# A graph attention layer with residual layer norm on one core: attention mixes x before gcn_w instead of after it

## The chip, the core and the metric

The kernel runs on one core of a Trainium2 chip. Its time is the time of one launch on the device, in microseconds (us). Times inside a launch come from one profiled execution; "the span" is the stretch from its first to its last instruction.

## The reference

There are 128 graphs of 64 nodes with 384 features each, x[128, 64, 384], and an integer matrix adj[128, 64, 64] with ones on the diagonal. For each graph, with the embedding row e = table[adj]:

```
hi = x @ W1[:384] + e @ W1[384:] + b1          # for each pair (i, j)
hj = x @ W2[:384] + e @ W2[384:] + b2
rel = sum(hi * hj);  A = softmax(where(adj != 0, rel, -1e9))
h   = relu((A @ x) @ gcn_w + gcn_b)
out = layernorm(x + h @ Wo + bo)
```

With adj only 0 or 1, the scores are x M x^T plus a term of the column, plus a term of the row u.x + k, where M, u and k are made once from the weights. A second, slower path in the kernel handles other values of adj; it does not run on these inputs and its few changed lines are left out below.

## The kernel before

The 8192 rows (tokens) are worked in 16 groups of 512: four pairs of graphs, 128 rows each. Every large product is made three times in a 4-byte format: a value is split into a high and a low part, and high x high, high x low and low x high are added in PSUM (`three`, L444). Before the loop come the weights: M = W1 W2^T (`m_stage`), the column term, the row term's column u (put beside gcn_w as columns 384 and 385 of `gcn_hi` and `gcn_lo`), and gcn_b laid out as a row by a matmul (`gb_row`).

TensorE's stages in a group are, in the order of `body`:
- `mix`: attention times the values of the group before, 96 matmuls of 64 columns; result in four banks;
- `score_stage`: 48 matmuls of 64 columns;
- `value` for the next group: x @ [gcn_w, u, u], 4 times 9 matmuls of 386 columns, which VectorE adds to gcn_b and stores as `hg_sb` (`value_out`);
- `out` of the group before: hidden rows times Wo, 4 times 9 matmuls of 384 columns;
- `turn`: transposes the attention weights;
- `proj` for the next group: M times x^T, 27 matmuls of 512 columns, which ScalarE stores as `gt_sb` (`project_out`).

ScalarE splits off the high part of relu(mixed) (`hidden`), takes the exponentials (`weigh`), splits x (`split_x`), copies the row terms (`row_terms`). VectorE makes the low part of the hidden rows (`low_half`), adds the row terms and the mask to the scores and takes maxima, normalises the weights, and at the end of each body adds x to the output, takes statistics (`residual`), moments (`moments`), and normalises (`normalise`). GpSimd adds bo to x (`bias_x`, L1140), makes the mask (`mask`, L1136), makes the low part of x (`split_x`, L1131) and takes mean and variance to 1/std (`inverse_std`: L1149, L1151). SyncE issues the loads and stores. Each queue is in order; the orders are written out by hand, and the engines meet by counting semaphores. The bodies 0, 1, 14 and 15 are unrolled with small differences; 2 to 13 are a loop of six double bodies.

Of the kernel before, what the change touches and what calls it, by code (L numbers as in the profile page):

```python
# [52 lines left out]
def gnn_layernorm_kernel(nc, x, x_t, adj, adj_t, edge, biases, w1_t, w2_t, gcn_w, wo_w, wo_b, out):  # L53
# [8 lines left out]
    HW = HID + 2  # L62
    ROW = HID + 64
# [16 lines left out]
    with ExitStack() as ctx:  # L80
# [10 lines left out]
        wo_lo = sb("wo_lo", [P, C, HID], F32R)  # L91
        sb("gap0", [P, 48])
# [4 lines left out]
        sb("gap1", [P, 32])  # L97
        gcn_hi = sb("gcn_hi", [P, C, ROW], F32R)[:, :, 0:HW]
        gcn_lo = sb("gcn_lo", [P, C, ROW], F32R)[:, :, 0:HW]
        ident = sb("ident", [P, P])  # L100
        w1t_sb = sb("w1t_sb", [P, C, HID])
        w2t_sb = sb("w2t_sb", [P, C, HID + 1])
# [4 lines left out]
        b1_sb, b2_sb, gb_sb = (bias_sb[:, n * C:(n + 1) * C] for n in range(3))  # L107
        wob_sb = sb("wob_sb", [P, HID])
# [13 lines left out]
        hg_sb = sb("hg_sb", [P, 2, PAIRS, HID + 1])  # L122
# [9 lines left out]
        gb_diag = sb("gb_diag", [P, HID])  # L132
        gb_row = sb("gb_row", [P, HID + 1])
# [30 lines left out]
        edges = sb("edges", [P, NODES])  # L164

# [3 lines left out]
        PROJ_BANK = [bank[4], bank[2], bank[3]]  # L169
        MIX_BANK = ((6, 6, 4), (7, 7, 5))  # L170
        VALUE_BANK = bank[1:5]
        score = bank[0]
        M_BANK = bank[5:8]
        PROJ0_BANK = bank[5:8]
        PROJ1_BANK = [bank[5], bank[2], bank[3]]
        C_BANK = bank[3], bank[4]
        GB_BANK = bank[2]
# [9 lines left out]
        gcn_loaded = [sem(f"gcn_loaded{c}") for c in range(C)]  # L187
# [4 lines left out]
        x_loaded = [sem(f"x_loaded{i}") for i in range(2)]  # L192
        adj_loaded = [sem(f"adj_loaded{i}") for i in range(2)]
# [13 lines left out]
        zero_column = sem("zero_column")  # L207
# [3 lines left out]
        gb_diag_ready = sem("gb_diag_ready")  # L211
        gb_mm = sem("gb_mm")
        gb_row_ready = sem("gb_row_ready")
# [12 lines left out]
        u_hi_ready = sem("u_hi_ready")  # L226
        u_lo_ready = sem("u_lo_ready")
# [10 lines left out]
        value_mm = sem("value_mm")  # L238
        hg_ready = sem("hg_ready")
# [7 lines left out]
        mix_mm = sem("mix_mm")  # L247
        hshi = sem("hshi")
        hslo = sem("hslo")
# [50 lines left out]
        def out_bank(g, q):  # L300

            if static(g, LAST - 2) and HALVES <= q:
                return bank[q - 1]
            if static(g, LAST - 1):
                return bank[(3, 1, 2, 3)[q]]
            if static(g, LAST):
                return bank[q + 1]
            return bank[(5, 6, 7, 1)[q]]
# [5 lines left out]
        def x_home(g, slot):  # L314

            if static(g, LAST):
                return xt_sb[:, 0].rearrange("p c t -> p (c t)").rearrange("p (q d) -> p q d", d=HID)
            return x_sb[:, slot]

        def y_home(g, slot):  # L320

            if static(g, LAST):
                return xt_sb[:, 1].rearrange("p c t -> p (c t)").rearrange("p (q d) -> p q d", d=HID)
            return y_sb[:, slot]
# [42 lines left out]
        def _(sp):  # L367
# [11 lines left out]
            sp.dma_start(xt_sb[:, 0, :, GT // 2:GT], xt_cols[0][:, :, GT // 2:GT]).then_inc(xt_loaded[0], 16)  # L379
            sp.dma_start(xt_sb[:, 1], xt_cols[1]).then_inc(xt_loaded[1], 16)  # L380
            sp.dma_start(wob_sb[:], wo_b.to_broadcast([P, HID])).then_inc(wob_loaded, 16)
            sp.dma_start(wo_sb[:], wo_w.rearrange("(c p) n -> p c n", p=P)).then_inc(wo_loaded, 16)
            load_adj(0, 0)
            load_adj(1, 1)
            sp.dma_start(x_sb[:, 0], x_rows[0]).then_inc(x_loaded[0], 16)

            def body(g, par):

                if before(g, GROUPS - 2):
# [6 lines left out]
                if not static(g, 0):  # L396
                    if before(g, LAST - 1):
# [852 lines left out]
```

## Time and profile before

| | |
|---|---|
| time, median of 3 runs | 381.94 us (381.56 to 383.81) |
| the profiled execution's own time | 381.69 us |
| its span | 379.6 us |
| TensorE busy (matmuls) | 371.9 us, 98% |
| VectorE, GpSimd, ScalarE busy | 220.3, 153.5, 142.6 us |
| granted clock of TensorE, mean | 0.998 |

A busy TensorE is counted from each matmul's start to its modelled end, and ends overlap the next start; so rates below are taken from starts, not from durations. The two microseconds between span and time lie around the profiled part.

### The profile page before, as it was taken

The numbers are of one execution on the slowest core, as the hardware profiler recorded it, in microseconds if no ns is written. First come the engines' busy times: TensorE is split into PE (matmuls) and PEld (weight loads), VectorE is DVE, ScalarE is ACT, GpSimd is POOL, SyncE is SP. The second block draws the span as 40 slices with busy tenths as digits, with TensorE's granted clock in tenths as the row PEclk, the third lists the DMA queues.
The fourth block names the chain that finished last, engine by engine and source line by source line (L and its number), as shares of the span: only waits on it lengthen the run. The fifth ranks groups of instructions, "written<-read, shape, count | busy, mean of one in ns | idle before, by whom it ended". The sixth has DMA issues, their size and how long they took to land.

```text
span 379.6 us, 10085 instructions
## 1 busy us (share of the span) xinstructions
PE 371.9 (98%) x4009; PEld 339.4 (89%) x4009; DVE 220.3 (58%) x584; ACT 142.6 (38%) x343; POOL 153.5 (40%) x134
## 2 busy tenths in 40 slices
PE   8999999999999999999999999999999999999992
PEld 4789898999989899998989999898999989898982
DVE  2546264675646467464656756465675646566694
ACT  1725442514334251433424243342523344133443
POOL 0333463270815427081541808144180714517044
PEclk9999999999999999999999999999999999999999
DMA  7922123408062350806225080522608053160114
GB/s 230 323 99 85 24 77 100 165 17 249 3 182 81 69 193 12 251 0 179 84 68 194 7 249 6 175 87 53 209 5 232 25 165 97 36 229 3 42 44 167
DMA packets 34852, 42.88 MB, mean 113 GB/s; under 512 B 10129, under 2 KB 29073, under 8 KB 34833
## 3 DMA queue, kind: packets, MB, share of 16 engines
q1 hardware_dynamic: 33744, 41.33, 36.2%
q10 hardware_dynamic: 1088, 1.29, 1.0%
q8 instruction: 13, 0.21, 0.2%
q14 instruction: 7, 0.05, 0.0%
HBM read 30.03 MB, written 12.58 MB: 112 GB/s over the span
## 4 chain that ended last, share of the span: by engine, by line
PE 98%; DVE 0%; POOL 0%; issue 0%
PE banks L446 18%; PE banks L448 18%; PE banks L447 18%; PE banks L545 9%; PE banks L539 9%; PE banks L540 9%; PE banks L525 7%; PE banks L470 7%; PE banks L563 2%; PE banks L552 1%; PE banks L505 1%; PE banks L573 0%; PE banks L589 0%; PE banks L584 0%; DVE stats L867 0%; DVE xt_sb L862 0%
## 5 line engine op out<-in xcount | busy, mean ns | idle before, releaser
L1140 POOL TENSOR_TENSOR x_sb<-x_sb,wob_sb 128x1536 f32<-128x1536 f32 x15 | 52.8, 3520 | 174.7 <-DVE weights L978 174.7
L947 DVE SCALAR_TENSOR_TENSOR hs_lo<-banks,hs_hi 128x256 fp32r<-128x256 f32 x90 | 32.6, 417 | 67.3 <-ACT hs_hi L809 67.2
L446 PE MATMUL banks<-gcn_hi,xt_hi 128*128 128x386 f32 x192 | 66.7, 347 | 0.0
L447 PE MATMUL banks<-gcn_lo,xt_hi 128*128 128x386 f32 x192 | 64.8, 338 | 0.0
L448 PE MATMUL banks<-gcn_hi,xt_lo 128*128 128x386 f32 x192 | 64.8, 338 | 0.0
L545 PE MATMUL banks<-wo_hi,hs_lo 128*128 128x384 f32 x180 | 60.8, 338 | 0.0
L539 PE MATMUL banks<-wo_hi,hs_hi 128*128 128x384 f32 x180 | 60.6, 337 | 0.0
L540 PE MATMUL banks<-wo_lo,hs_hi 128*128 128x384 f32 x180 | 60.5, 336 | 0.0
L750 ACT ACTIVATE gt_sb<-banks,r_sb 128x512 f32<-128x512 f32 x48 | 33.1, 689 | 69.6 <-PE banks L448 69.5
L446 PE MATMUL banks<-xt_hi,m_hi 128*128 128x512 f32 x144 | 57.4, 398 | 0.0
L448 PE MATMUL banks<-xt_hi,m_lo 128*128 128x512 f32 x144 | 56.8, 394 | 0.0
L447 PE MATMUL banks<-xt_lo,m_hi 128*128 128x512 f32 x144 | 56.4, 392 | 0.0
L1131 POOL TENSOR_TENSOR xt_lo<-xt_sb,xt_hi 128x1536 fp32r<-128x1536 f32 x15 | 52.8, 3521 | 0.7 <-ACT xt_hi L744 0.7
L862 DVE TENSOR_TENSOR y_sb<-banks,x_sb 128x384 f32<-128x384 f32 x60 | 33.3, 556 | 28.4 <-PE banks L545 28.4
L852 DVE TENSOR_TENSOR hg_sb<-banks,gb_row 128x385 f32<-128x385 f32 x64 | 34.4, 555 | 22.0 <-PE banks L448 22.0
L446 PEld LDWEIGHTS banks<-gcn_hi,xt_hi 128*128 128x128 f32 x192 | 36.2, 189 | 1.1
L447 PEld LDWEIGHTS banks<-gcn_lo,xt_hi 128*128 128x128 f32 x192 | 36.3, 189 | 0.0
L799 ACT ACTIVATE prob<-rel,nmax 128x64 f32<-128x64 f32 x64 | 21.5, 337 | 39.5 <-DVE nmax L966 39.5
L448 PEld LDWEIGHTS banks<-gcn_hi,xt_lo 128*128 128x128 f32 x192 | 36.3, 189 | 0.0
L867 DVE BATCH_NORM_STATS2 stats<-y_sb 128x6 f32<-128x384 f32 x60 | 33.6, 560 | 2.0
L545 PEld LDWEIGHTS banks<-wo_hi,hs_lo 128*128 128x128 f32 x180 | 33.8, 188 | 0.7 <-DVE hs_lo L947 0.7
L539 PEld LDWEIGHTS banks<-wo_hi,hs_hi 128*128 128x128 f32 x180 | 33.9, 188 | 0.1
(97 smaller groups left out, 512.7 us busy)
## 6 DMA issues: line engine op xcount, KB each, us to landing
xt_sb<-in_x_t_dram SPq DMA_DIRECT2D x15, 768.0 KB, 4.6
x_sb<-in_x_dram SPq DMA_DIRECT2D x15, 768.0 KB, 5.6
out_dram<-y_sb SPq DMA_DIRECT2D x30, 384.0 KB, 5.9
adj_sb<-in_adj_dram SPq DMA_DIRECT2D x32, 64.0 KB, 2.3
xt_sb<-in_x_t_dram SPq DMA_DIRECT2D x2, 384.0 KB, 8.8
xt_sb<-in_x_dram SPq DMA_DIRECT2D x1, 768.0 KB, 5.9
out_dram<-xt_sb SPq DMA_DIRECT2D x4, 192.0 KB, 2.1
w1t_sb<-in_w_t_dram ACTq DMA_DIRECT2D x3, 192.0 KB, 6.2
```

The lines of the kernel that those rows point to most:

```text
L446: pe.matmul(acc, a_hi, b_hi, start=first, stop=False)
L447: pe.matmul(acc, a_hi, b_lo, start=False, stop=False)
L448: return pe.matmul(acc, a_lo, b_hi, start=False, stop=last)
L539: pe.matmul(acc, hs_home(g)[0][:, c, ts], wo_hi[:, c, :], start=(c == BLOCKS[0]), stop=False)
L540: pe.matmul(acc, hs_home(g)[0][:, c, ts], wo_lo[:, c, :], start=False, stop=False)
L545: mm = pe.matmul(out_bank(g, q)[:, 0:HID], hs_home(g)[1][:, c, ts], wo_hi[:, c, :], start=False, stop=(c == BLOCKS[-1]))
L750: act.activation(gt_sb[:, f, :], of[f][:, 0:GT], ACT.Identity, bias=r_sb[:, f:f + 1]).then_inc(gt_ready, 1)
L852: dve.tensor_tensor(hg_sb[:, slot, q, :], VALUE_BANK[q][:, 0:HID + 1], gb_row[:], ALU.add).then_inc(hg_ready, 1)
L862: dve.tensor_tensor(y_home(g, slot)[:, q, :], out_bank(g, q)[:, 0:HID], x_home(g, slot)[:, q, :], ALU.add).then_inc(added, 1)
L867: dve.bn_stats(stats[:, q, :], y_home(g, slot)[:, q, :]).then_inc(statd, 1)
L1131: pool.tensor_tensor(xt_lo[:, slot], xt_sb[:, slot], f32(xt_hi[:, slot]), ALU.subtract).then_inc(xlo, 1)
L1140: pool.tensor_tensor(x_home(g, slot), x_home(g, slot), wob_sb[:].rearrange("p (o n) -> p o n", o=1).to_broadcast([P, PAIRS, HID]), ALU.add ...
```

## The change

The order of the two products is exchanged: attention first mixes the rows of x themselves (`x_sb` in `mix`), giving z = A x in transposed form; z is split into `z_hi` and `z_lo` (ScalarE `split_z`, VectorE `low_z`); then gcn_w is applied as 27 matmuls of 512 columns (`gemm`) with z^T streaming. gcn_b is now a per-partition bias in ScalarE's relu (`hidden`); the low part of the hidden rows takes a second ScalarE pass (`less_sb`) and one VectorE pass (`low_hidden`). u.x is no longer a column of a matmul but four products with a running sum on VectorE (`row_products`). x is loaded twice: into `x_sb` for mixing and into `y_sb` for the residual, where bo is added in place. `gemm` comes after the mix, so its operands depend on it, and `out` of a group moves: three of its four parts stand at the end of the next body, the fourth in the body after that, ahead of `gemm`. With it `residual` of part 3, `moments`, `inverse_std`, `normalise` and the stores of a group move one body later, and `normalise` now stands ahead of `low_hidden` on VectorE; `inverse_std` stands ahead of `bias_x` on GpSimd. At the start, the load of gcn_w moves to SyncE's queue and into one DMA, x of group 0 and the first mask are loaded ahead of x^T of group 1, wo's low part is made on GpSimd, u is laid out as a row by three matmuls, gcn_b's row and u's columns fall away, and `proj(1)` is begun before `score_stage(0)`.

The core of the diff (the queue of each line is the first word of its calls):

```diff
+            return bank[(1, 2, 3, 1)[q]]
+        def gemm_bank(g):
+            return [bank[2], bank[4], bank[5]] if static(g, LAST) else GEMM_BANK
...
+                if not static(g, 0) and before(g, LAST):
+                    sp.wait_ge(mix_mm, g)
+                    sp.dma_start(x_sb[:, 1 - par], x_rows[g + 1]).then_inc(x_loaded[1 - par], 16)
...
+                    sp.wait_ge(y_ready, HALVES * (g - 2) + h + 1)
+                    sp.dma_start(out_rows[g - 2][:, 2 * h:2 * h + 2], y_sb[:, par, 2 * h:2 * h + 2]).then_inc(stored[par], 16)
+                sp.wait_ge(stored[par], 1 + 16 * HALVES * half(g, par))
+                sp.dma_start(y_sb[:, par], x_rows[g]).then_inc(y_loaded[par], 16)
...
-            def value(g, par, q):
...
+            def gemm(g):
+                for f in range(C):
+                    fs = slice(f * P, (f + 1) * P)
+                    if static(g, LAST):
+                        pe.wait_ge(added, PAIRS * (g - 1))
+                    elif not (static(g, 0) or static(g, LAST - 1) and f == C - 1):
+                        pe.wait_ge(added, PAIRS * (g - 1) + f + 2)
+                    for n, c in enumerate(BLOCKS):
+                        if f == 0:
+                            pe.wait_ge(zlo, C * g + n + 1)
+                        mm = three(gemm_bank(g)[f][:, 0:GT], gcn_hi[:, c, fs], gcn_lo[:, c, fs],
+                                   z_hi[:, c, :], z_lo[:, c, :], n == 0, n == C - 1)
+                    mm.then_inc(gemm_mm, 1)
...
-                pe.wait_ge(hg_ready, PAIRS * (g + 1))
...
+                if static(g, 0):
+                    pe.wait_ge(gt_ready, C)
+                elif not static(g, LAST):
+                    pe.wait_ge(gt_ready, C * (g + 2))
...
+            def out(g, q):
+                if q < HALVES or static(g, LAST):
+                    pe.wait_ge(hslo, C * (g + 1))
+                if static(g, LAST) and q < HALVES:
+                    pe.wait_ge(added, PAIRS * (g - 1) + q + 1)
+                elif q == PAIRS - 1 and static(g, LAST - 2):
+                    pe.wait_ge(hslo, C * (g + 1) + 1)
+                elif q == PAIRS - 1 and before(g, LAST - 2):
+                    pe.wait_ge(added, PAIRS * g + 1)
...
+            proj(0, 0)
+            pe.wait_ge(xlo, 2)
+            proj(1, 1, PROJ1_BANK, range(2))
...
             def body(g, par):
                 if not static(g, 0):
                     mix(g - 1, 1 - par)
                 score_stage(g, par)
+                if static(g, 0):
+                    proj(1, 1, PROJ1_BANK, range(2, C * C - 1))
+                    pe.wait_ge(ident_ready, 1)
+                    turn(g)
+                    proj(1, 1, PROJ1_BANK, range(C * C - 1, C * C))
+                    return
+                if static(g, 1):
+                    pe.wait_ge(gcn_lo_ready, 1)
+                elif static(g, LAST):
+                    out(g - 2, 2)
+                else:
+                    out(g - 2, 3)
+                gemm(g - 1)
+                turn(g)
                 if static(g, LAST):
-                    out(g - 2, (2, 3))
-                    out(g - 1, (0, 1))
-                    turn(g)
-                    out(g - 1, (2,))
+                    out(g - 2, 3)
                     mix(g, par)
-                    out(g - 1, (3,))
+                    out(g - 1, 0)
+                    out(g - 1, 1)
+                    gemm(g)
+                    out(g - 1, 2)
+                    out(g - 1, 3)
+                    for q in range(PAIRS):
+                        out(g, q)
                     return
-                for q in range(PAIRS):
...
+                pe.wait_ge(xlo, g + 2)
+                proj(g + 1, 1 - par)
+                if static(g, 1):
+                    pe.wait_ge(wo_lo_ready, 1)
+                for q in range(2 if static(g, LAST - 1) else PAIRS - 1):
+                    out(g - 1, q)
...
+            def split_z(g):
                 act.wait_ge(mix_mm, g + 1)
                 for n, f in enumerate(BLOCKS):
                     if n == C - 1:
-                        act.wait_ge(hslo, C * g + 1)
-                    act.activation(by_graph(hs_home(g)[0][:, f, :]), mixed(f), ACT.Relu).then_inc(hshi, 1)
+                        act.wait_ge(zlo, C * g + 1)
+                    act.copy(by_graph(z_hi[:, f, :]), mixed(f)).then_inc(zhi, 1)
+            def hidden(g):
+                if static(g, 0):
+                    act.wait_ge(ngb_ready, 1)
+                else:
+                    act.wait_ge(hslo, C * g)
+                for f in range(C):
+                    act.wait_ge(gemm_mm, C * g + f + 1)
+                    act.activation(hs_home(g)[0][:, f, :], gemm_bank(g)[f][:, 0:GT], ACT.Relu,
+                                   bias=gb_sb[:, f:f + 1]).then_inc(hshi, 1)
+                    act.wait_ge(hshi, C * g + f + 1)
+                    act.activation(less_sb[:, f, :], f32(hs_home(g)[0][:, f, :]), ACT.Identity,
+                                   bias=ngb_sb[:, f:f + 1]).then_inc(less_ready, 1)
             def body(g, par):
                 if not static(g, 0):
-                    hidden(g - 1)
+                    split_z(g - 1)
                 weigh(g)
                 if before(g, LAST - 1):
                     split_x(g + 2, par)
-                if before(g, LAST):
-                    row_terms(g + 1, 1 - par)
+                if not static(g, 0):
+                    hidden(g - 1)
                 act.wait_ge(turn_mm, g + 1)
                 act.copy(at_sb[:], score[:, 0:MIX]).then_inc(at_ready, 1)
                 if before(g, LAST):
                     project_out(g + 1, PROJ1_BANK if static(g, 0) else PROJ_BANK)
+                    row_terms(g + 1)
                 else:
+                    split_z(g)
+                    normalise_last(LAST - 2, 1, 1, (0, 1))
+                    normalise_last(LAST - 2, 1, 1, (2, 3))
                     hidden(g)
...
+            def row_products(g, slot):
+                dve.wait_ge(x_loaded[slot], 16 * (half(g, slot) + 1))
+                if not static(g, 0):
+                    dve.wait_ge(srow_ready, g)
+                for q in range(PAIRS):
+                    a = dve.scalar_tensor_tensor(products[:, q, :], x_sb[:, slot, q, :], 1.0, u_row[:], ALU.mult, ALU.mult,
+                                                 accum_out=xu_row[:, q:q + 1])
+                a.then_inc(xu_ready, 1)
...
+            def low_z(g):
+                for n, f in enumerate(BLOCKS):
+                    dve.wait_ge(zhi, C * g + n + 1)
                     for h in range(HALVES):
-                        a = dve.scalar_tensor_tensor(by_graph(hs_home(g)[1][:, f, :])[:, h], mixed(f)[:, h], 0.0,
-                                                     by_graph(f32(hs_home(g)[0][:, f, :]))[:, h], ALU.max,
-                                                     ALU.subtract)
-                    a.then_inc(hslo, 1)
+                        a = dve.tensor_tensor(by_graph(z_lo[:, f, :])[:, h], mixed(f)[:, h],
+                                              by_graph(f32(z_hi[:, f, :]))[:, h], ALU.subtract)
+                    a.then_inc(zlo, 1)
+            def low_hidden(g, f):
+                dve.wait_ge(less_ready, C * g + f + 1)
+                dve.scalar_tensor_tensor(hs_home(g)[1][:, f, :], gemm_bank(g)[f][:, 0:GT], ngb_sb[:, f:f + 1],
+                                         less_sb[:, f, :], ALU.max, ALU.subtract).then_inc(hslo, 1)
...
-                elif static(g, 0):
-                    value_out(1, 1, 0)
-                    value_out(1, 1, 1)
+                    residual(g - 2, par, 2)
+                elif not (static(g, 0) or static(g, 1)):
+                    residual(g - 2, par, 3)
+                    dve.wait_ge(statd, PAIRS * (g - 1))
+                if static(g, 0):
+                    dve.wait_ge(max_zero, 1)
                 else:
-                    value_out(g + 1, 1 - par, 0)
-                    value_out(g + 1, 1 - par, 1)
+                    dve.wait_ge(adjmax, g)
+                most(par)
+                if not (static(g, 0) or static(g, 1) or static(g, LAST)):
+                    moments(g - 2, range(PAIRS))
                 dve.wait_ge(expd, g + 1)
                 dve.reciprocal(rsum[:], psum_row[:]).then_inc(normed, 1)
                 dve.wait_ge(normed, 2 * g + 1)
                 dve.tensor_tensor(weights[:], prob[:], rsum[:].rearrange("p (q o) -> p q o", o=1)
                                   .to_broadcast([P, PAIRS, NODES]), ALU.mult).then_inc(normed, 1)
                 if static(g, LAST):
-                    statistics(g - 2, par, 2)
...
                     dve.wait_ge(adjmax, GROUPS)
                     dve.tensor_reduce(row_max[:], adj_max[:], AX_XY, ALU.max).then_inc(rowmax_ready, 1)
-                    low_half(g, range(C))
...
+                elif not (static(g, 0) or static(g, 1)):
+                    for h in range(HALVES):
+                        normalise(g - 2, par, g - 1, (2 * h, 2 * h + 1))
+                if not static(g, 0):
+                    for f in range(C):
+                        low_hidden(g - 1, f)
+                if before(g, LAST):
+                    row_products(g + 1, 1 - par)
+                    if not static(g, 0):
+                        for q in range(2 if static(g, LAST - 1) else PAIRS - 1):
+                            residual(g - 1, 1 - par, q)
...
+                if not (static(g, 0) or static(g, 1) or static(g, LAST)):
+                    inverse_std(g - 1, g - 2, slice(0, PAIRS))
+                pool.wait_ge(normed, 2 * (g + 1))
+                if before(g, LAST):
+                    pool.wait_ge(adj_loaded[1 - par], 32 * (half(g + 1, 1 - par) + 1))
+                if not static(g, 0):
+                    bias_x(g - 1, 1 - par)
                 if static(g, LAST):
-                    inverse_std(g - 2, 1, slice(2, 4))
-                    shift(g - 2, 1, (2, 3))
+                    bias_x(g, par)
+                    inverse_std(g - 1, g - 2, slice(0, PAIRS))
+                    shift(g - 1, g - 2, range(PAIRS))
                     for h in range(HALVES):
-                        inverse_std(g - 1, h, slice(2 * h, 2 * h + 2))
-                        shift(g - 1, h, (2 * h, 2 * h + 1))
+                        inverse_std(g + h, g - 1, slice(2 * h, 2 * h + 2))
+                        shift(g + h, g - 1, (2 * h, 2 * h + 1))
                     return
-                pool.wait_ge(normed, 2 * (g + 1))
-                pool.wait_ge(adj_loaded[1 - par], 32 * (half(g + 1, 1 - par) + 1))
-                bias_x(g, par)
                 mask(g + 1, 1 - par)
                 if before(g, LAST - 1):
                     split_x(g + 2, par)
-                else:
...
```

## Rows read from the trace of the kernel before

**Rows 1.** The page: the chain of work that ended last, shares by engine
```profile
PE 98%; DVE 0%; POOL 0%; issue 0%
```
**Rows 2.** Busy time of each engine in one whole group, mix to mix
```profile
198.39:220.66 22.27, 22.27 (x247) 20.70 (x246) 13.19 (x35) 8.22 (x20) 9.37 (x7) 1.00 0.36 111
```
**Rows 3.** Timeline of TensorE, the first row of each stage: start, us, line, operands
```profile
198.39 1.63 PE L525 MATMUL banks<-at_sb,hg_sb 64*64 64x64 f32 x96
199.95 1.62 PE L470 MATMUL banks<-xt_sb,gt_sb 128*64 128x64 f32 x48
201.50 0.45 PE L446 MATMUL banks<-gcn_hi,xt_hi 128*128 128x386 f32 x1
...
207.91 0.34 PE L539 MATMUL banks<-wo_hi,hs_hi 128*128 128x384 f32 x1
...
214.15 0.38 PE L505 MATMUL banks<-ident,weights 128*128 128x128 f32 x2
214.29 0.48 PE L446 MATMUL banks<-xt_hi,m_hi 128*128 128x512 f32 x1
...
220.33 0.40 PE L448 MATMUL banks<-xt_hi,m_lo 128*128 128x512 f32 x1
```
**Rows 4.** Timeline of TensorE at the start of the kernel
```profile
8.52 0.91 PE L589 MATMUL banks<-gb_diag,ones 128*128 128x384 f32 x2
9.36 0.52 PE L595 MATMUL banks<-c_sb,w1t_sb 128*64 128x1 f32 x12
9.80 4.15 PE L563 MATMUL banks<-w2t_sb,w1t_sb 128*128 128x385 f32 x12
...
15.08 0.45 PE L446 MATMUL banks<-gcn_hi,xt_hi 128*128 128x386 f32 x1
```
**Rows 5.** Timeline of ScalarE and VectorE in the group of rows 3
```profile
200.09 1.09 ACT L809 ACTIVATE hs_hi<-banks 128x512 fp32r<-128x512 f32 x2 [0.90 <-PE banks L525]
...
205.86 0.19 ACT L799 ACTIVATION_READ_ACCUMULATOR prob<-rel,nmax 128x1 f32 x1
206.28 1.48 ACT L744 CAST xt_hi<-xt_sb 128x1536 fp32r<-128x1536 f32 x1 [0.23 <-DMA xt_sb<-in_x_t_dram]
...
200.72 2.18 DVE L947 SCALAR_TENSOR_TENSOR hs_lo<-banks,hs_hi 128x256 fp32r<-128x256 f32 x6 [4.65 <-ACT hs_hi L809]
...
204.15 0.42 DVE L966 TENSOR_REDUCE nmax<-rel 128x4 f32<-128x256 f32 x1
...
206.29 0.43 DVE L978 TENSOR_TENSOR weights<-prob,rsum 128x256 f32<-128x256 f32 x1
```
**Rows 6.** Groups of instructions, whole kernel: busy, mean ns of one, idle before
```profile
L862 DVE TENSOR_TENSOR y_sb<-banks,x_sb 128x384 f32<-128x384 f32 x60 | 33.3, 556 | 28.4 <-PE banks L545 28.4
L867 DVE BATCH_NORM_STATS2 stats<-y_sb 128x6 f32<-128x384 f32 x60 | 33.6, 560 | 2.0
L750 ACT ACTIVATE gt_sb<-banks,r_sb 128x512 f32<-128x512 f32 x48 | 33.1, 689 | 69.6 <-PE banks L448 69.5
```
**Rows 7.** Durations of single lines of GpSimd, min/median/max
```profile
L1149 POOL TENSOR_TENSOR veps<-mv,eps_sb x34: 190/201/340, 58.4 to 374.2; 128x2 f32<-128x2 f32 x30, 128x1 f32<-128x1 f32 x4
L1151 POOL TENSOR_TENSOR rstd<-veps,mhalf x34: 550/702/817, 58.6 to 374.5; 128x2 f32<-128x2 f32 x30, 128x1 f32<-128x1 f32 x4
```
**Rows 8.** Timeline of GpSimd and VectorE where long GpSimd operations overlap VectorE's
```profile
34.30 3.51 POOL L1140 TENSOR_TENSOR x_sb<-x_sb,wob_sb 128x1536 f32<-128x1536 f32 x1 [11.82 <-DVE weights L978]
36.69 1.40 DVE L939 TENSOR_TENSOR adj_max<-adj_max,adj_sb 128x256 int32<-128x256 int32 x1
37.78 0.59 POOL L1136 TENSOR_SCALAR neg_sb<-adj_sb 128x256 f32<-128x256 int32 x1
...
17.48 3.53 POOL L1131 TENSOR_TENSOR xt_lo<-xt_sb,xt_hi 128x1536 fp32r<-128x1536 f32 x1 [0.66 <-ACT xt_hi L744]
...
19.39 2.82 DVE L933 TENSOR_TENSOR wo_lo<-wo_sb,wo_hi 128x1152 fp32r<-128x1152 f32 x1
```
**Rows 9.** Timeline of all engines around one group's normalisation
```profile
193.27 0.43 DVE L939 TENSOR_TENSOR adj_max<-adj_max,adj_sb 128x256 int32<-128x256 int32 x1
193.61 0.24 DVE L876 BATCH_NORM_AGGREGATE mv<-stats 128x2 f32<-128x6 f32 x2
193.77 0.84 DVE L884 TENSOR_SCALAR y_sb<-y_sb,mv,rstd 128x384 f32<-128x384 f32 x2
...
193.93 0.34 POOL L1149 TENSOR_TENSOR veps<-mv,eps_sb 128x2 f32<-128x2 f32 x1 [0.88 <-DVE mv L876]
194.35 0.81 POOL L1151 TENSOR_TENSOR rstd<-veps,mhalf 128x2 f32<-128x2 f32 x1
```

More of the change, by code:

```diff
@@ L192, in gnn_layernorm_kernel @@
         x_loaded = [sem(f"x_loaded{i}") for i in range(2)]
+        y_loaded = [sem(f"y_loaded{i}") for i in range(2)]
+        y_last_loaded = sem("y_last_loaded")
         adj_loaded = [sem(f"adj_loaded{i}") for i in range(2)]
@@ L448, in three, with proj @@
                 return pe.matmul(acc, a_lo, b_hi, start=False, stop=last)
-            def proj(g, par, into=PROJ_BANK):
-                if not (static(g, 0) or static(g, 1)):
-                    pe.wait_ge(hg_ready, PAIRS * (g + 1))
-                for f in range(C):
-                    if static(g, 1) and 0 < f:
-                        pe.wait_ge(hg_ready, PAIRS + f + 1)
+            def proj(g, par, into=PROJ_BANK, parts=range(C * C)):
+                for part in parts:
+                    f, c = part // C, part % C
                     fs = slice(f * P, (f + 1) * P)
-                    for c in range(C):
-                        mm = three(into[f][:, 0:GT], m_hi[:, c, fs], m_lo[:, c, fs],
-                                   xt_hi[:, par, c, :], xt_lo[:, par, c, :], c == 0, c == C - 1)
-                    mm.then_inc(proj_mm, 1)
+                    mm = three(into[f][:, 0:GT], m_hi[:, c, fs], m_lo[:, c, fs],
+                               xt_hi[:, par, c, :], xt_lo[:, par, c, :], c == 0, c == C - 1)
+                    if c == C - 1:
+                        mm.then_inc(proj_mm, 1)
             def score_stage(g, par):
@@ L1009, in body @@
                 dve.wait_ge(statd, PAIRS * (g - 1) + 2)
-                if whole:
-                    residual(g - 1, 1 - par, 2)
-                    moments(g - 1, (0, 1))
-                    residual(g - 1, 1 - par, 3)
-                    dve.wait_ge(statd, PAIRS * g)
-                dve.wait_ge(adjmax, g)
-                most(par)
-                moments(g - 1, (2, 3) if whole else (0, 1))
-                normalise(g - 1, 1 - par, 1, (0, 1))
-                if whole:
-                    normalise(g - 1, 1 - par, 2, (2, 3))
+                moments(g - 1, (0, 1))
+                for f in range(C):
+                    low_hidden(g, f)
+                residual(g - 1, 1 - par, 2)
+                residual(g - 1, 1 - par, 3)
+                dve.wait_ge(statd, PAIRS * g)
+                moments(g - 1, (2, 3))
             run(dve, body)
```

364 lines of the change are left out of this document (113 added, 251 removed).

## The prediction

> **What bounds the kernel.** I read the chain of work that ended last first: TensorE has 98% of it [rows 1]. One group, cut out of the steady part, shows the same: TensorE is busy for all 22.27 us at full granted clock (1.00, the 2.4 GHz level), VectorE for 13.19, GpSimd for 9.37, ScalarE for 8.22 [rows 2]. So the kernel costs TensorE's columns, and the other engines matter only where one of them is late. The starts of the stages give what each takes: mix 1.56, score 1.55, value 6.41, out 6.24, turn 0.14, proj 6.37 (to the group's end at 220.66, rows 2) [rows 3].
>
> **The TensorE terms.** The change swaps value, 36 matmuls of 386 columns in 6.41 us, for gemm, 27 of 512, the very shape of proj. Proj's first and last start are 6.04 apart, so one takes 0.232 and 27 of them 6.27; with proj's own switch into the mix it is 6.37. The gain is 0.04 to 0.24 a group; I take 0.15, or 2.4 us over 16. Why so little: the columns are 13,824 against 13,896, and only the fixed part of nine matmuls goes. The Trainium skill (VectorE: DVE Perf Modes, the table under the TRN2 errata) gives a matmul max(60, 6 + columns) cycles at 2.4 GHz; by it the gain would be 0.05 us a group, under 1 us in all. The starts are further apart than that rule says, and I go by the starts.
>
> **The start.** Removed: gb_diag's matmul and the twelve matmuls of one column, 8.52 to 9.80, 1.3 us. Added: u as a row, three matmuls of 384 columns; six of 385 took 4.15, so 2.1 [rows 4]. Net +0.8: the groups' work begins at 15.9 instead of 15.08. Then the pipeline fills differently: gemm(0) can't start before mix(0). I follow it with the durations of the stages and copies [rows 3, 5, 6]. proj(0) ends at 22.1, six matmuls of proj(1) at 23.5, score(0) at 25.1, eighteen more at 29.2. weights come 5.15 us after a score's end (206.72 against 201.57) [rows 3, 5], less some 1.3 for low_half, which group 0 doesn't have ahead of them, so turn(0) just doesn't wait. Then ScalarE stands in split_x(2) until x^T has landed: 206.28, 4.7 us after the score, and 1.5 for the copy; at_sb only then: 31.7, while TensorE is through at 30.1, 1.6 idle. score(1) waits for three copies of 0.69, 0.6; ScalarE then has row_terms, and z starts late, 1.1. Together 3.3 us idle, once; bounds 1 (if the orders mesh better) and 7 (the second load of x, 2 x 768 KB, delays wo or x^T). At the end the same chain follows the last out; I take 0.3 for at_sb behind hidden(14), bounds -1.5 and +2.
>
> So far: -2.4 + 0.8 + 3.3 + 0.3 = +2.0.
>
> **The steady group: which waits stay hidden.** Let S be a score's end. The order is then out(g-2, 3) to S+1.6, gemm(g-1) to S+7.9, turn, proj to S+14.3, three parts of out to S+19.0, mix, score.
> - z: mix ends at S-1.55; high and low parts go out in the pattern of hs_hi and hs_lo now, the last low 2.9 us after mix's end [rows 5], at S+1.3, and gemm begins at S+1.6 and takes them one by one. Hidden by score and out(g-2, 3); without these it would cost 1.5.
> - turn: nmax ends at S+3.0, residual part 3 at S+4.15 (0.556 + 0.560) [rows 6], the adj maximum at S+4.5, four moments at S+4.95 (0.12 each) [rows 9], weights at S+5.6. turn is at S+7.9: 2.3 of cover.
> - at_sb, gt, row_terms on ScalarE: weigh ends at S+4.5, split_x by S+6.2 to 9 (two other loads now ahead of it), hidden with its second pass 3 x (0.69 + 0.6), so S+10.1 to 13; mix needs at_sb at S+19. Hidden. Loads: x_sb and y_sb each have most of a group to land. Cost 0.
> - row_products: four of 384; the nearest rows say 0.56 each, a doubling 1.1. It ends before out's parts do, and its effect is 0 at both ends.
> - low_hidden must be done by S+14.3, as out(g-1, 0) waits for all three. Three of 512 columns, about 0.65 each by ScalarE's 0.69 and hs_lo's 0.36 for 256. Behind ScalarE alone it is done at S+13.3 or so.
>
> **The step that fails.** Ahead of low_hidden on VectorE stands normalise(g-2), ahead of that the wait for rstd. GpSimd gets moments at S+5.0, needs 0.20 + about 1.0 (0.70 for two columns) [rows 7], and rstd is there at S+6.2. GpSimd goes straight on to bias_x, 3.5 us, mask, 0.4, and split_x, 3.5, since normed has been set at S+5.6. Before, GpSimd's long operations were over when normalise ran. Do they disturb each other? The trace shows what such an operation does to a VectorE one with two SBUF inputs [rows 8]: adj_max took 1.40 instead of 0.43 and ended 0.28 after GpSimd's; wo_lo took 2.82 and ended 1.20 after, 1152 elements' worth. They wait for the whole operation. normalise has one SBUF input, and no row puts it beside a long operation. But veps, 0.20 elsewhere, takes 0.34 when it falls into normalise, and rstd 0.81 for 0.70 [rows 7, 9]: it is exclusive too. And veps came through between two normalises, as mask came after adj_max and not before: the two sides alternate.
> The Trainium skill (SBUF — State Buffer, Terms) says of this shared port pair that it is "Lock-allocated, exclusive, held for the full instruction"; the trace agrees for two inputs [rows 8], and for one input it has no more than [rows 9].
> So: bias_x to S+9.8, normalise 1 to 10.1, mask to 10.4, normalise 2 to 10.7, split_x to 14.1, normalise 3 and 4 to 14.75, low_hidden to 16.7. If VectorE wins the first turn, bias_x is second and split_x still stands ahead of normalise 4: the same. TensorE waits from S+14.3: 2.3 us a group, bounds 1.7 and 3.0. It happens where normalise, bias_x and split_x all stand in the body, bodies 2 to 13: 12 x 2.3 = 27.6, bounds 20 and 36. Body 14 has no split_x. What is behind it, out, mix and score, moves by the same amount, so nothing heals it.
>
> **Sum.** 379.6 + 2.0 + 27.6 = 409.2 of span; 2.1 lie around the profiled span (381.69 less 379.6): 411.3. The median shown is 0.25 above the profiled time, nothing beside this. I say 411.
>
> **Rivals.**
> - VectorE keeps the port, or gets it back, for all four normalises after bias_x (or isn't held at all): low_hidden is then done at S+13.3, TensorE never waits, and 379.6 + 2.0 + 2.1 = 383.7, +0.5%, bounds 380 and 388. For it: 1 us of cover is left, and only two small operations tell of the alternation. It decides where the last normalise ends before S+12.3. Chance 0.22.
> - The start meshes as well as before and the port costs nothing: 2.4 saved, less 0.8: 380.1; faster by over 1% only if matmul starts of gemm came closer than proj's. Against: one stage of that very shape [rows 3]. Chance 0.03 for under 378.1.
> - The wait is longer than three: x^T lands late, as y_sb's load and x_sb's load stand ahead of it, ScalarE's hidden slips past S+15 as well, or VectorE's residuals delay z: 3.5 to 4 a group, 425 to 432. Against: DMA was busy 0.36 of a group [rows 2] and a third load makes half. Chance 0.07.
> - That the columns don't fall: they fall by 0.5%, which is why this part can't pay for any wait.
> My forecast has 0.68.
>
> **Range and chances.** A change within 1% (378.1 to 385.8) is about what a measurement can't tell from none. The forecast's own range is 403 to 420. To leave out no more than 2 in 10 it must reach the first rival: 382 to 420. Slower by over 1%: 0.68 + 0.07 and the upper end of the first rival, 0.03: 0.78. Within 1%: 0.19. Faster: 0.03.
>
> **What would show it.** In the trace after: gemm's matmuls 0.23 apart; TensorE idle some 2.3 us in each of twelve groups ahead of out(g-1, 0), released by VectorE's hs_lo; TensorE's share near 91%; two of the four normalises starting only when split_x ends, or one of them lasting 3.5 us; a group of 24.4 us. Right but for the port: a group of 22.1 and no normalise over 0.5 us. Wrong otherwise: an idle ahead of gemm (z late) or ahead of turn (weights late), or of mix (at_sb).

## The result and the profile after

The changed kernel takes 416.45 us (median of 4 runs, 415.69 to 418.4) against 382.88 for the kernel before beside it (4 runs): a ratio of 1.088, 95% interval 1.082 to 1.095. The profiled execution took 415.69, its span is 413.9. The forecast was 411, in a range of 382 to 420.

Work on each engine in the page's first part, then the clock line (40 slices, tenths of full speed), and the chain of work that ended last, by engine:

```profile
PE 379.4 (92%) x3857; PEld 325.3 (79%) x3857; DVE 329.7 (80%) x684; ACT 201.5 (49%) x435; POOL 147.9 (36%) x108
...
PEclk9999999999998999999899999989999998999999
...
PE 42%; DVE 37%; issue 10%; POOL 4%; ACT 3%; DMA 3%; ACTq 0%; DVEq 0%; POOLq 0%
```

TensorE had 98% of the chain before [rows 1]; now VectorE has 37%, though it is busy for only 80% of the span. An engine with time to spare that stands on the chain is one that others wait for. The groups of instructions (busy, mean ns of one, idle before and its releaser) say with what, and the list of waits says who pays:

```profile
L865 DVE TENSOR_SCALAR y_sb<-y_sb,mv,rstd 128x384 f32<-128x384 f32 x52 | 102.5, 2029 | 11.9 <-POOL rstd L1115 11.9
```
```profile
PE banks L452 <- DVE hs_lo L918: 24.7, 12, 2.1
ACT xt_hi L711 <- DMA xt_sb<-in_x_t_dram: 24.5, 14, 2.7
```

Two normalises together took 0.84 before [rows 9]; they overlap a little, and one alone lasts 0.45 to 0.48. The mean of one is 2.03 now. TensorE waits twelve times, 2.1 at most. The second line is the load of x^T, which ScalarE waits for: 24.5 us in all where there were 5.9 before; an experiment below tells what hangs on it. One group of the changed kernel, GpSimd, VectorE and ScalarE around the normalises (start, us, engine, line; a row with "x4" runs from the first start to the last end). The score's end, the S of the prediction, is 206.94:

```profile
212.09 1.07 POOL L1115 TENSOR_TENSOR rstd<-veps,mhalf 128x4 f32<-128x4 f32 x1
213.14 3.51 POOL L1105 TENSOR_TENSOR y_sb<-y_sb,wob_sb 128x1536 f32<-128x1536 f32 x1
213.20 8.14 DVE L865 TENSOR_SCALAR y_sb<-y_sb,mv,rstd 128x384 f32<-128x384 f32 x4 [0.91 <-POOL rstd L1115]
213.37 1.48 ACT L711 CAST xt_hi<-xt_sb 128x1536 fp32r<-128x1536 f32 x1 [1.97 <-DMA xt_sb<-in_x_t_dram]
216.63 0.51 POOL L1098 TENSOR_SCALAR neg_sb<-adj_sb 128x256 f32<-128x256 int32 x1
217.11 3.62 POOL L1093 TENSOR_TENSOR xt_lo<-xt_sb,xt_hi 128x1536 fp32r<-128x1536 f32 x1
218.13 0.72 ACT L784 ACTIVATE less_sb<-hs_hi,ngb_sb 128x512 f32<-128x512 f32 x1
221.26 2.06 DVE L918 SCALAR_TENSOR_TENSOR hs_lo<-banks,ngb_sb,less_sb 128x512 fp32r<-128x512 f32 x3
```

The row "x4" is the four normalises together. One by one, their own rows say which of GpSimd's operations each meets:

```profile
213.20 3.68 DVE L865 TENSOR_SCALAR y_sb<-y_sb,mv,rstd 128x384 f32<-128x384 f32 x1 [0.91 <-POOL rstd L1115]
216.80 0.56 DVE L865 TENSOR_SCALAR y_sb<-y_sb,mv,rstd 128x384 f32<-128x384 f32 x1
217.27 3.67 DVE L865 TENSOR_SCALAR y_sb<-y_sb,mv,rstd 128x384 f32<-128x384 f32 x1
220.87 0.47 DVE L865 TENSOR_SCALAR y_sb<-y_sb,mv,rstd 128x384 f32<-128x384 f32 x1
```

The first is held until `bias_x` has ended (216.65), the second runs around the mask, the third is held until `split_x` has ended (220.73), the fourth is free: the turns of the prediction.

The same group on TensorE, the first row of each stage:

```profile
208.54 0.39 PE L452 MATMUL banks<-z_hi,gcn_hi 128*128 128x512 f32 x1
...
214.72 0.38 PE L500 MATMUL banks<-ident,weights 128*128 128x128 f32 x2
214.86 0.48 PE L452 MATMUL banks<-xt_hi,m_hi 128*128 128x512 f32 x1
...
220.92 0.39 PE L454 MATMUL banks<-xt_hi,m_lo 128*128 128x512 f32 x1
...
223.37 0.45 PE L452 MATMUL banks<-wo_hi,hs_hi 128*128 128x384 f32 x1 [2.06 <-DVE hs_lo L918]
...
228.25 1.63 PE L519 MATMUL banks<-at_sb,x_sb 64*64 64x64 f32 x96
```

The matmul due at 221.15 (220.92 and 0.23) starts at 223.37: 2.22 late. ScalarE's last `less_sb` ended at 218.85, so it is VectorE alone that is late. There are twelve such waits, of 2.02 to 2.08, in bodies 2 to 13, and none in body 14.

And something of which the prediction had said nothing. Four stretches, just behind the waits that end at 172.84, 197.33, 272.32 and 347.3 (busy time of the five engines, then the granted clock as a share of full speed, the DMA share, GB/s). The first is one of the eight behind which nothing happens:

```profile
172.84:176.30 3.46, 3.46 (x20) 3.46 (x21) 3.01 (x11) 1.17 (x4) 0.00 (x0) 1.00 0.36 103
198.50:201.70 3.20, 3.20 (x11) 3.20 (x11) 1.80 (x6) 1.17 (x4) 0.00 (x0) 0.50 0.81 222
273.70:276.90 3.20, 3.20 (x11) 3.20 (x11) 1.60 (x4) 1.17 (x4) 0.00 (x0) 0.50 0.78 239
348.60:351.80 3.20, 3.20 (x12) 3.20 (x11) 1.67 (x6) 1.17 (x4) 0.00 (x0) 0.50 0.79 221
```
```profile
198.12 0.33 PE L453 MATMUL banks<-wo_lo,hs_hi 128*128 128x384 f32 x1
198.29 0.41 PE L454 MATMUL banks<-wo_hi,hs_lo 128*128 128x384 f32 x1
198.50 0.52 PE L452 MATMUL banks<-wo_hi,hs_hi 128*128 128x384 f32 x1
198.82 0.52 PE L453 MATMUL banks<-wo_lo,hs_hi 128*128 128x384 f32 x1
```

About 1.1 us after TensorE took up work again behind the wait ending at 197.33, its clock fell to half, the 1.2 GHz level, and the output matmuls stand 0.32 apart instead of 0.17. The lower level lasts 3.4 us, from 198.4 to 201.8. This happens four times, from 123.3, 198.4, 273.5 and 348.6 on, behind every third wait. The group between 197.33 and 223.37 takes 26.04; one without it, from 203.76 to 228.25, takes 24.49.

### The profile page after: what moved, and what is told of

Same layout as the page of the kernel before. It is cut to its first block, busy times and chain, and to the rows that moved or that the text cites. A ratio compares the mean times of both kernels' runs of the same rounds, so it can differ in the third digit from the quotient of the medians.

```text
span 413.9 us, 9956 instructions
## 1 busy us (share of the span) xinstructions
PE 379.4 (92%) x3857; PEld 325.3 (79%) x3857; DVE 329.7 (80%) x684; ACT 201.5 (49%) x435; POOL 147.9 (36%) x108
## 4 chain that ended last, share of the span: by engine, by line
PE 42%; DVE 37%; issue 10%; POOL 4%; ACT 3%; DMA 3%; ACTq 0%; DVEq 0%; POOLq 0%
DVE y_sb L865 17%; PE banks L452 12%; PE banks L453 11%; PE banks L454 11%; DVE hs_lo L918 6%; PE banks L519 6%; DVE z_lo L911 5%; POOL rstd L1115 3%; DVE rel L929 2%; ACT z_hi L771 2%; DVE stats L848 2%; DVE y_sb L843 2%; DMA w1t_sb<-in_w_t_dram 1%; DVE rel L933 1%; DVE adj_max L904 1%
## 5 line engine op out<-in xcount | busy, mean ns | idle before, releaser
L865 DVE TENSOR_SCALAR y_sb<-y_sb,mv,rstd 128x384 f32<-128x384 f32 x52 | 102.5, 2029 | 11.9 <-POOL rstd L1115 11.9
L452 PE MATMUL banks<-wo_hi,hs_hi 128*128 128x384 f32 x180 | 66.1, 367 | 24.7 <-DVE hs_lo L918 24.7
L1105 POOL TENSOR_TENSOR y_sb<-y_sb,wob_sb 128x1536 f32<-128x1536 f32 x15 | 52.6, 3508 | 21.8 <-DVE weights L951 21.8
L452 PE MATMUL banks<-z_hi,gcn_hi 128*128 128x512 f32 x144 | 56.5, 393 | 1.0 <-DVE z_lo L911 1.0
L453 PE MATMUL banks<-z_lo,gcn_hi 128*128 128x512 f32 x144 | 56.7, 394 | 0.0
L771 ACT CAST z_hi<-banks 128x512 fp32r<-128x512 f32 x48 | 26.6, 589 | 61.5 <-PE banks L519 56.2
L454 PE MATMUL banks<-z_hi,gcn_lo 128*128 128x512 f32 x144 | 56.0, 389 | 0.0
L911 DVE TENSOR_TENSOR z_lo<-banks,z_hi 128x256 fp32r<-128x256 f32 x96 | 34.6, 418 | 18.6 <-ACT z_hi L771 18.6
L843 DVE TENSOR_TENSOR y_sb<-banks,y_sb 128x384 f32<-128x384 f32 x60 | 33.3, 555 | 18.4 <-PE banks L454 18.3
L918 DVE SCALAR_TENSOR_TENSOR hs_lo<-banks,ngb_sb,less_sb 128x512 fp32r<-128x512 f32 x45 | 31.2, 739 | 7.8 <-ACT less_sb L784 7.8
L834 DVE SCALAR_TENSOR_TENSOR onehot<-x_sb,u_row 128x384 f32<-128x384 f32 x64 | 37.1, 632 | 0.0
```

What stands on the lines that cost most here:

```text
L452: pe.matmul(acc, a_hi, b_hi, start=first, stop=False)
L453: pe.matmul(acc, a_hi, b_lo, start=False, stop=False)
L454: return pe.matmul(acc, a_lo, b_hi, start=False, stop=last)
L771: act.copy(by_graph(z_hi[:, f, :]), mixed(f)).then_inc(zhi, 1)
L834: a = dve.scalar_tensor_tensor(products[:, q, :], x_sb[:, slot, q, :], 1.0, u_row[:], ALU.mult, ALU.mult, accum_out=xu_row[:, q:q + 1])
L843: dve.tensor_tensor(y_home(g, slot)[:, q, :], out_bank(g, q)[:, 0:HID], y_home(g, slot)[:, q, :], ALU.add).then_inc(added, 1)
```

## The experiments

The theory: GpSimd's long operations (`bias_x`, `split_x`) and VectorE's normalise exclude each other and take turns, so that both long ones run before the last normalise; low_hidden stands behind it, TensorE waits for that, and the clock falls after some of the waits. Each kernel is the changed one with one edit (those of "The start" have two). Where an edit leaves work out, the result is not that of the layer, and the kernel is there for its time alone.

**low_hidden ahead of the normalises.** All the work stays; only VectorE's order changes.

```diff
-                elif not (static(g, 0) or static(g, 1)):
-                    for h in range(HALVES):
-                        normalise(g - 2, par, g - 1, (2 * h, 2 * h + 1))
                 if not static(g, 0):
...
                         low_hidden(g - 1, f)
+                if not (static(g, 0) or static(g, 1) or static(g, LAST)):
+                    for h in range(HALVES):
+                        normalise(g - 2, par, g - 1, (2 * h, 2 * h + 1))
```

> The order of VectorE's queue alone: low_hidden ahead of normalise in every body. Port theory (normalise waits for GpSimd's bias_x and split_x, and low_hidden stands behind it): TensorE's twelve waits of 2.2 us (26.6) go, and the four dips of the granted clock behind them (6.0) too: about 384 us. The normalises still last 8 us together, now with nobody behind them but row_products. Rival (VectorE, 80% busy, has simply too much to do): the wait moves from out to another stage, ahead of gemm or of mix, and at least half of it stays: 398 or more.

Measured: 380.99 (10 runs), 0.999 of before (0.996 to 1.001), span 378.3. No wait of TensorE in the groups, and no fall of the clock. In one thing the expectation missed: the four normalises take not 8 us but 1.88 (224.24 to 226.12), as `split_x` is nearly over when they start. Two rows of one group, VectorE and GpSimd:

```profile
221.19 3.53 POOL L1093 TENSOR_TENSOR xt_lo<-xt_sb,xt_hi 128x1536 fp32r<-128x1536 f32 x1
222.23 0.75 DVE L918 SCALAR_TENSOR_TENSOR hs_lo<-banks,ngb_sb,less_sb 128x512 fp32r<-128x512 f32 x1 [0.58 <-ACT less_sb L784]
```

low_hidden, which reads a PSUM bank and one tile of SBUF, runs at 0.75 in the middle of the 3.53 of `split_x`: it is not held. So it needs only to stand ahead of what is. The whole loss, 35.6 us of span (413.9 less 378.3), hangs on that order. What the rest of the change is worth comes out as 378.3 against 379.6, from one profiled execution each; the timings side by side, 380.99 and 381.94 with an interval that holds 1, don't show it to be more than none.

**Each long operation cut away.** In one kernel `bias_x` adds 8 columns of its 1,536, in the other `split_x` from body 2 on does.

```diff
-                pool.tensor_tensor(y_home(g, slot), y_home(g, slot),
-                                   wob_sb[:].rearrange("p (o n) -> p o n", o=1).to_broadcast([P, PAIRS, HID]),
+                pool.tensor_tensor(y_home(g, slot)[:, 0, 0:8], y_home(g, slot)[:, 0, 0:8], wob_sb[:, 0:8],
                                    ALU.add).then_inc(xb, 1)
```

> GpSimd's bias_x is cut to 8 columns of one pair, so bo is not added to x; VectorE's queue and work are as they were. Port theory: only split_x (3.5 us) is left in normalise's way, the last normalise ends some 3.5 us earlier, at S+11 (S: the end of a score), low_hidden by S+13, and TensorE doesn't wait: 384 us. Rival (too much work on VectorE): no change, 414 to 418.

```diff
                 if before(g, LAST - 1):
-                    split_x(g + 2, par)
+                    if static(g, 0) or static(g, 1):
+                        split_x(g + 2, par)
+                    else:
+                        pool.wait_ge(xhi, g + 3)
+                        pool.tensor_tensor(xt_lo[:, par, 0, 0:8], xt_sb[:, par, 0, 0:8], f32(xt_hi[:, par, 0, 0:8]),
+                                           ALU.subtract).then_inc(xlo, 1)
```

> GpSimd's split_x in the bodies from 2 on is cut to 8 columns of one block, so the low part of x^T stays that of groups 2 and 3; VectorE's queue and work are as they were. Port theory with the two sides taking turns: bias_x alone delays the first normalise to S+9.8, the other three follow behind mask: done by S+11.5, low_hidden by S+13.5, no wait: 384 us. If the two sides did not take turns (VectorE barred until GpSimd's whole queue is empty) the same would come out here, but then the first normalise lasts 4 us or more in the trace. Rival (too much work on VectorE): 414 to 418.

Measured: 382.86 and 381.6 (one run each). Neither has a wait in the groups. The normalises of the second, with the long operation beside them:

```profile
218.85 3.51 POOL L1105 TENSOR_TENSOR y_sb<-y_sb,wob_sb 128x1536 f32<-128x1536 f32 x1
218.91 4.92 DVE L865 TENSOR_SCALAR y_sb<-y_sb,mv,rstd 128x384 f32<-128x384 f32 x4 [0.92 <-POOL rstd L1115]
```

The four normalises still take 4.92, 3.3 more than the 1.65 that they take undisturbed (below), and TensorE doesn't wait. The first of them lasts 3.67, to the end of `bias_x` and not to that of the short operations behind it, which would have made it over 4: GpSimd doesn't keep VectorE out until its queue is empty. The cover that its projection gives is enough for one long operation and not for two.

**The length of the operation.** `bias_x` on two of the four pairs, and on three (`[:, 0:2]` and `[:, 0:3]` of y in the same call); and, the other way, a second addition of 1,152 columns, into a spare tile, behind the whole `bias_x` of bodies 2 to 14:

```diff
+                if not isinstance(g, int) or 1 <= g <= LAST - 2:
+                    pool.tensor_tensor(spare_sb[:], gcn_sb[:], wo_sb[:], ALU.add)
```

> The changed kernel, but bias_x treats two of its four pairs (bo is not added to the others). bias_x lasts 1.8 us instead of 3.5, all else in place. Port theory: the last normalise ends 1.7 us earlier, TensorE waits 0.5 instead of 2.2 in twelve bodies: 20 us less. If the dips of the granted clock come from the waits' length they go as well, 6 us: 390; if they come from having any wait, 396.

> GpSimd's addition of the bias runs on three of the four pairs (the output of the fourth lacks the bias). Between half of it (waits of 0.4 us, no dips, 389.0) and all of it (2.05 us and four dips, 416.5) the port theory puts the wait at 1.2 us in each of 12 groups: 389.0 + 12 x 0.83 = 399 with the clock at its upper level throughout, up to 405 if the dips come as with the whole addition. Rival: the normalises are held by a fixed round of turns and not by the length of the addition; then the wait jumps to one of its neighbours, 389 or 410 and more.

> The changed kernel and one more GpSimd addition of 1152 columns into a spare tile behind bias_x in bodies 2 to 14, on tiles that nobody waits for; it adds nothing to VectorE's queue. Port theory: it takes a turn of its own between two normalises, 2.7 us; the last normalise, low_hidden and out follow 2.7 later in twelve bodies, body 14 waits about 1.2: 416.4 + 33.6 = 450 us, and more if the clock dips more often. Rival (too much work on VectorE, or ScalarE late): no change, 416.

Measured, one run each: 389.02, 398.6 and 467.96 (expected 390, 399 and 450). The list of waits of the three kernels, in that order:

```profile
PE banks L452 <- DVE hs_lo L918: 4.8, 12, 0.4
```
```profile
PE banks L452 <- DVE hs_lo L918: 14.8, 12, 1.2
```
```profile
PE banks L453 <- DVE hs_lo L919: 53.7, 13, 4.4
```

With 1.85, 2.68 and 3.51 us of addition the wait is 0.40, 1.23 and 2.06: each microsecond that GpSimd works longer is a microsecond that TensorE waits, from an addition of some 1.45 on (1.85 less 0.40). The rival of a fixed round of turns is gone. The 2.81 of the extra addition bring 2.3 a group, to 4.37, where 2.7 was expected. The turns say why: with one operation more on GpSimd, one normalise more gets through ahead of the end of `split_x`, and only the last of the four, held in its turn, ends behind it. In one group of that kernel:

```profile
212.74 10.44 DVE L866 TENSOR_SCALAR y_sb<-y_sb,mv,rstd 128x384 f32<-128x384 f32 x4 [0.92 <-POOL rstd L1118]
216.15 2.81 POOL L1110 TENSOR_TENSOR spare_sb<-gcn_sb,wo_sb 128x1152 f32<-128x1152 f32 x1
219.41 3.55 POOL L1094 TENSOR_TENSOR xt_lo<-xt_sb,xt_hi 128x1536 fp32r<-128x1536 f32 x1
```

The four last 3.67, 2.85, 0.56 and 3.60, and the last ends 0.22 behind `split_x` (223.18 and 222.96); in the changed kernel the third ends there and the fourth 0.4 later. The time of that kernel went well beyond the waits, mostly because of the clock. The same columns as above for one group of the kernel with three pairs, and in two stretches of the kernel with the extra addition, just behind waits:

```profile
190.35:214.00 23.65, 22.42 (x237) 19.40 (x237) 20.59 (x43) 11.78 (x26) 8.00 (x5) 1.00 0.44 139
```
```profile
225.80:228.90 3.10, 3.10 (x11) 3.10 (x10) 1.89 (x8) 1.17 (x4) 0.00 (x0) 0.50 0.55 144
254.10:259.50 5.40, 5.40 (x19) 5.40 (x18) 2.44 (x8) 1.17 (x4) 0.00 (x0) 0.50 0.45 146
```

Behind waits of 0.4 and 1.2 us the clock never fell; behind 2.06 it fell every third time; behind 4.4 every time, for 3.4 us in six groups and for 6.8 in the other six, and in eight of the twelve it fell within the wait already. In the last kernel the work done at the lower level behind these twelve waits takes 53.9 us, which at 0.17 us a matmul instead of 0.32 would be some 29.3: 24.6 us lost to the clock, against 6.2 in the changed kernel. Of the 52 us of span that separate the two (466.1 less 413.9), the twelve waits longer by 2.3 make 28 and the clock behind them 18. The rest is a wait of 1.22 in body 14 (about 1.2 was expected) and, at the start, a wait for z_lo of 3.07 instead of 0.95 with a 13th fall of the clock.

**The handover.** GpSimd waits for the four normalises before it starts `bias_x`; nothing else changes.

```diff
                     pool.wait_ge(adj_loaded[1 - par], 32 * (half(g + 1, 1 - par) + 1))
+                if not (static(g, 0) or static(g, 1) or static(g, LAST)):
+                    pool.wait_ge(y_ready, HALVES * (g - 1))
                 if not static(g, 0):
                     bias_x(g - 1, 1 - par)
```

> All work and VectorE's order as they were; GpSimd waits for the count that normalise has reached before bias_x. Port theory: normalise runs alone, four times 0.47 with starts 0.38 apart, done by S+8; bias_x, mask and split_x end at S+15.5; low_hidden is ready behind ScalarE, S+13; no wait of TensorE: 384 us. row_products now meets split_x and lasts up to 3 us longer, which its place hides. Rival (too much work on VectorE): no change, 414 to 418.

Measured: 380.44 (11 runs), 0.995 of before (0.993 to 0.997). Since this would be a kernel faster than both, it was timed again:

> The same kernel as e4_port_handover, timed again in more rounds: GpSimd waits for the four normalises before its addition of the bias in bodies 2 to 14. Its first timing stood at 0.995 of the kernel before (0.993 to 0.997). If that holds, 380 to 381 and an interval wholly below 1; if it was a chance of the runs, 382 and an interval that holds 1. No wait of TensorE in the groups, and none of the dips behind the out products, in either case.

Measured: 382.34 (12 runs), 1.001 (0.999 to 1.003), span 379.2. The first interval was not borne out: this version is level with the kernel before, and no more is shown. Its mechanism is clear, though. VectorE and GpSimd in one group:

```profile
218.40 1.65 DVE L865 TENSOR_SCALAR y_sb<-y_sb,mv,rstd 128x384 f32<-128x384 f32 x4 [0.91 <-POOL rstd L1115]
220.21 3.53 POOL L1105 TENSOR_TENSOR y_sb<-y_sb,wob_sb 128x1536 f32<-128x1536 f32 x1 [1.84 <-DVE y_sb L865]
```

Four normalises in 1.65 instead of 8.14. A wait of 1.84 was added to GpSimd and took 2.06 from TensorE. As expected, the first of `row_products` now meets `split_x` and lasts 3.65; TensorE doesn't wait for it.

**The loads.** The second load of x in the loop, cut to 8 columns.

```diff
-                sp.dma_start(y_sb[:, par], x_rows[g]).then_inc(y_loaded[par], 16)
+                sp.dma_start(y_sb[:, par, 0, 0:8], x_rows[g][:, 0, 0:8]).then_inc(y_loaded[par], 16)
```

> The second load of x in the loop is cut to 8 of its 1,536 columns, so that the y it feeds holds wrong values and the output is not the reference's; 13 loads of 786 KB are gone, every operation on the engines stays. Port theory: the loads are covered, the wait ahead of the out product stays at 2.05 us in each of 12 groups, the four dips of the clock stay, and the time is that of the changed kernel, 414 to 418. ScalarE's wait for x^T (24.5 us over 14 groups) shrinks toward the 5.9 of before and moves nothing. Rival: the later x^T and with it GpSimd's split of x is what holds the normalise longer; then the waits shrink and the time is 410 or less.

Measured: 416.87 (one run), and the same twelve waits of 2.04 to 2.08. ScalarE's wait for x^T only went from 24.5 to 21.8, so the expected fall toward 5.9 was wrong: the second load is not what makes x^T late, and what does stays open. The clock fell five times here, behind the waits ending at 73.4, 99.4, 198.9, 273.9 and 349.0: "every third" is how it came out in the changed kernel and no rule.

**The start.** The split of x for group 2 one body later, on top of low_hidden first, and on top of the handover.

```diff
+                if static(g, 1):
+                    split_x(2, 0)
                 weigh(g)
-                if before(g, LAST - 1):
+                if before(g, LAST - 1) and not static(g, 0):
                     split_x(g + 2, par)
```

> low_hidden ahead of normalise (as in e1_low_first), and ScalarE's split_x(2) moved from body 0 to body 1, behind split_z(0), so that at_sb(0), the copies of proj(1) and z of group 0 no longer stand behind the landing of x^T. The theory of the start says that 1.1 us ahead of mix(0) and 1.0 ahead of gemm(0) go: 379 us against e1's 380.99. Rival: x^T of group 2 is then late for proj(2), or weigh(1) for turn(1), and it comes out as e1 or above, 381 to 382.

> GpSimd waits for normalise before bias_x (as in e4_port_handover), and the start as in e6_low_first_start. 378.4 us against e4's 380.44 if the start's idle goes; 380.5 if it only moves.

Measured: 381.93 and 381.36 (12 runs each), 1.000 of before both (0.997 to 1.002 and 0.997 to 1.003). The wait for at_sb ahead of mix(0) is gone, but that for z_lo stays at 0.95, and a new one of 0.34 stands ahead of a turn. Body 2's mix starts at 52.88 in the first, where it started at 52.90 without the edit: nothing was gained, against the expectation of 379 and 378.4. The second expectation had named the outcome of an idle that only moves, 380.5.

## Why the prediction was right, step by step

**The port step.** Right in its mechanism and nearly in each time. After S = 206.94: rstd was forecast at S+6.2 and came at 6.2; bias_x to 9.8, measured 9.7; split_x to 14.1, measured 13.8; the last normalise to 14.75, measured 14.4; low_hidden to 16.7, measured 16.4. TensorE's wait came out at 2.22 against 2.3, in exactly the bodies 2 to 13. A group with it takes 24.49, one without (low_hidden first) 22.15: 2.34, of which 0.1 is the slower first matmul after a stop (0.28 to the next start). So 12 x 2.34 = 28.1 against 27.6. The Trainium skill (SBUF — State Buffer, Terms) calls the shared port pair locked, exclusive and held for a full instruction; the runs agree, and for an operation with one SBUF tensor (and two per-partition scalars) as input too. The durations of single normalises (ns, min/median/max) in the changed kernel and in the one with the handover:

```profile
L865 DVE TENSOR_SCALAR y_sb<-y_sb,mv,rstd x52: 464/559/3685, 63.2 to 367.6; 128x384 f32<-128x384 f32 x52
```
```profile
L865 DVE TENSOR_SCALAR y_sb<-y_sb,mv,rstd x52: 472/476/483, 63.3 to 330.3; 128x384 f32<-128x384 f32 x52
```

The longest is as long as a long operation of GpSimd (3.51 to 3.62) and a little.

**gemm for value.** gemm takes 6.18 (208.54 to 214.72) where value took 6.41 [rows 3]. The whole group gave 0.12 back, 22.27 [rows 2] to 22.15: forecast 0.15. Sixteen of them, 1.9 against 2.4. The sum of the prediction left a term out: `out`, now in two pieces, takes 0.19 more (4.77 and 1.66 with low_hidden first, 6.24 before [rows 3]), which eats most of gemm's 0.23; proj gave 0.08.

**The start and the end.** proj(0) starts at 16.02, forecast 15.9; with low_hidden first, where no load of the weights was late, it is 15.46. TensorE then waits three times, 0.27, 0.89 and 0.95:

```profile
30.00 0.41 PE L500 MATMUL banks<-ident,weights 128*128 128x128 f32 x2 [0.27 <-DVE weights L951]
32.01 1.63 PE L519 MATMUL banks<-at_sb,x_sb 64*64 64x64 f32 x96 [0.89 <-ACT at_sb L797]
36.23 0.47 PE L452 MATMUL banks<-z_hi,gcn_hi 128*128 128x512 f32 x1 [0.95 <-DVE z_lo L911]
```

2.1 in all against 3.3 forecast. at_sb came when it was forecast to (31.7, measured 32.0), but TensorE was through with its work only at 31.1 and not at 30.1, and the 0.6 ahead of score(1) did not appear. From the last matmul's start to the end of the span there were 7.05 us before (372.55 to 379.6) and are 5.5 now (408.38 to 413.9): -1.5 where I had +0.3, at the lower bound given. Why it is shorter was not tried. All in all the change without the port costs -1.3 (378.3 less 379.6, one execution each), where I had +2.0.

**What the prediction missed.** The clock. Each fall adds 1.55 to its group (26.04 less 24.49), four of them 6.2. Nothing in the trace of before could show it, as TensorE never waited there; but the forecast put twelve waits into an engine that had stood at full clock without one [rows 2], and priced them at their length alone. A price for it was in no row, and the range took none in. The sum now: 379.6 - 1.3 + 28.1 + 6.2 + 0.8 for the later loads at the start (mix(0) at 32.01 against 31.22 with low_hidden first) = 413.4, of 413.9.

The forecast (411) is thus right in kind, with two misses of opposite sign: the clock, +6.2, and all that is outside the port step, -2.5 (-0.5 with the later loads, where I had +2.0). That they partly cancel is luck: with the clock alone the sum would have been 417.5.

**The rivals.** That VectorE gets the port for all four, or isn't held at all (383.7), is refuted by the rows of the normalises, 3.68 and 3.67 beside the long operations; the low-first and handover kernels, 381 and 380 to 382, show about what it would have cost. That the change would gain over 1% (under 378.1) came in none of the kernels without the wait either. The longer wait, 3.5 to 4 a group from late loads, did not come; the loads moved nothing when cut.

## What to carry to other kernels

Before an operation is moved on one engine, lay its place in time beside the long operations of the engine that shares its port: here four operations that take 1.65 us together grew to 8.14 because two of 3.5 fell in between. If they must meet, put the work that the bound engine waits for ahead of the one that is held, or let the other engine wait for a moment; either is a few lines, and here either brought the time back to that of the kernel before. And price a wait put into a saturated TensorE above its length: the restart and the clock made 34 us of twelve waits of 2.06 (24.7).

## What the hardware showed beyond that

- VectorE's normalise, which reads and writes SBUF only, with two per-partition scalars, is held by GpSimd's long operations (up to 3.69 us instead of 0.45 to 0.48), and the two sides take turns instruction by instruction (3.68, 0.56, 3.67, 0.47 in one group). `row_products`, with two SBUF inputs, likewise: 3.88 instead of 0.55 beside the split at the start. low_hidden, with one input in PSUM, is not held (0.75).
- TensorE's granted clock fell to the lower level after stops of 2.06 us in 4 of 12 cases (5 of 12 in the kernel with the cut load), after none of 0.40 or 1.23, and after all twelve of 4.4. In the kernels with 2.06 it fell not in the stop but 0.3 to 1.5 us into the work behind it, each time for 3.4 us; with 4.4 it fell in the stop or up to 0.5 us behind it, for 3.4 or 6.8. What decides which stops are followed by a fall stays open.
- A small wait of 1.84 us on the engine with slack (GpSimd, 36% busy) was free.
